# Three stacked attention layers on one core: score products of four heads together, opening work moved to GpSimd, maxima turned in half-height tiles

## The chip, the cores and the metric
The kernel runs on one core of one Trainium2 chip. The metric is the device time of one execution in microseconds (us), the median over the runs. TensorE (PE in the profile) multiplies, VectorE (DVE), ScalarE (ACT) and GpSimd (POOL) do the rest, and SyncE (SP) issues the transfers.

## The reference
One input x of 8 batches, 256 rows, 160 columns, and one context of 8 batches, 512 rows, 256 columns, pass through:

```
layer 0:  q = x Wq^T, k/v from the first 77 context rows (text) and, with other weights, from the other 435 (ip)
          20 heads of width 8, softmax over the text keys and over the ip keys apart, the two results added
          x = (text + ip) Wo^T + bo + x
layer 1:  n = layernorm(x) ; x = x + self_attention(n)         20 heads of width 64, 256 keys
          n = layernorm(x) ; x = x + cross_attention(n, ctx)   20 heads of width 64, 512 keys
          n = layernorm(x) ; x = x + (a * gelu(gate)) W2 + b2  with h = n W1 + b1 = (a, gate)
```

All in fp32. Products that need it are made of high and low parts (x = hi + lo, each rounded for one pass of TensorE).

## The kernel before, in words
The program is written engine by engine, without a scheduler: each engine walks its own list, and semaphores tie them. Four stages follow one another: layer 0 (`narrow_attention_layer`, tag l0, names `l_`), self attention (`self_attention_layer`, a1), cross attention (a2), feed forward (ff). The profile writes `a_` for a1 and for a2.

**Layer 0** takes 40 steps t: 8 batches b of 5 groups u, a group being four heads. A step has four parts s = 0 to 3. The pipeline is three deep: in step t the scores of group t are made (`score`, L1511), the exponentials of group t-2 are prepared from turned scores (`turned_scores`, L1526, then `exp` on ScalarE, L1705), and group t-3 is multiplied with the values (`weighted_sums`, L1593). A head's keys and queries lie in 32 partitions, so one score product is 32 rows by 128 queries by 512 keys. Part s makes one query tile (s // 2) of one pair of heads (s % 2): two products side by side into the two banks of `pscores[s % 2]`. VectorE reduces them to maxima (`maximum`, L1820, two reductions a part: text keys and ip keys), after which those banks are free: `score(g, s)` waits for `max_done` of the part two before it. After the four parts the maxima are turned by TensorE (`turn_max`, L1605, in part 2 of the next step) and placed into the queries by VectorE (`place_max`, L1827), between its maxima of parts 2 and 3. `PLAN` and `FIRST_PLAN` say in which parts the projections of the next batch are made (`project`, parts 1 and 3; names q, ip, text, rest, v0 to v3), and where the output of a finished batch is made ("out", part 1 of u = 2). `finish` spreads the reciprocals of a batch's sums in three pieces s0, s1, s2 (L1611), multiplied by VectorE (L1840); `invert` (L1834) makes the reciprocals, in part 3 of u = 3. Two batches ahead GpSimd splits the inputs (`split_inputs`, L1925 to L1928) and rounds the stacked keys and queries of the group three steps ahead (`round_stack`, L1951 and L1952); VectorE subtracts one small piece of it, 32 rows by 256 (`low_rest`, L1772, in part 1 of u = 4).

**Before the first step** all eight projections of batch 0 are made, in a bank each (`FIRST`).

**The opening of a1** runs in the last ten steps of layer 0 (OPEN = step 30): its weights are split into high parts (ScalarE, L595), low parts (GpSimd, L773) and the low rows of the rest (VectorE, L679), and the first layernorm is made (statistics and bias on VectorE, scaled by ScalarE). All three weights are loaded from step 24.

**Self attention** takes 40 steps d as well. In each, TensorE makes queries and keys (L514), scores (L472), turned scores (L492 to L498), weighted sums (L541, L546), turns the maxima (`turn_max`, L563: two transposes of 128 by 128 into one bank) and makes the values (L523). ScalarE copies the turned maxima into `neg_t` (`place_max`).

The tiles' places in memory are a table of addresses (`AT`).

## Time and profile before

| | us |
|---|---|
| median of 3 runs | 1612.28 |
| the three runs | 1616.55, 1592.74, 1612.28 |
| the profiled execution | 1618.48 |
| its span in the trace | 1616.7 |
| TensorE busy in it | 1544.4 (96%) |
| VectorE busy | 1106.0 (68%) |
| ScalarE busy | 776.6 (48%) |
| GpSimd busy | 419.1 (26%) |
| mean granted clock of TensorE | 0.959 |

Layer 0 fills the span from the start to about 385 us, self attention to about 800 us, cross attention to about 1530 us, feed forward the rest. Busy TensorE means that one of its instructions was open, not that the array worked at its peak. The granted clock is a share of 2.4 GHz; a stretch stands at 1.0 or at 0.5 (1.2 GHz), and a window over both shows a mean.

### The profile page before, as it was taken

What the parts mean: (1) busy time and instruction counts of PE and PEld (TensorE: products, weight loads), DVE (VectorE), ACT (ScalarE), POOL (GpSimd) and SP (SyncE); (2) the same over time, 40 slices, a digit from 0 to 9 for tenths busy, and PEclk for the clock granted to TensorE, in tenths of its full rate; (3) what the DMA queues carried; (4) which work ended last, traced back from release to release, by engine and by line L of the source; (5) the groups of instructions that cost most, each with busy time, mean ns of one, the idle gap of its engine ahead of it and who ended that gap; (6) DMA issues with size and microseconds to landing.
All of it is one profiled execution on the core that took longest, in us unless ns stands there. A gap on an engine that the chain in (4) does not pass through costs nothing.

```text
span 1616.7 us, 40554 instructions
## 1 busy us (share of the span) xinstructions
PE 1544.4 (96%) x17808; PEld 1206.9 (75%) x17808; DVE 1106.0 (68%) x1531; ACT 776.6 (48%) x1062; POOL 419.1 (26%) x375
## 2 busy tenths in 40 slices
PE   7999999998999999999999999999999999999988
PEld 5666656654788888788777877878887887877788
DVE  6777777655677777667567667676667667676666
ACT  4665656555445544556335444444444444443433
POOL 3333323320123222334312212221122222121300
PEclk7999989658999999999999999999999999999999
DMA  5322241100000020000201010101000020000000
GB/s 154 90 58 57 58 153 41 41 3 2 22 2 2 2 92 2 6 2 2 53 22 28 2 28 2 28 2 28 2 1 28 2 70 2 2 2 1 2 13 20
DMA packets 27211, 45.50 MB, mean 28 GB/s; under 512 B 7393, under 2 KB 15521, under 8 KB 26657
## 3 DMA queue, kind: packets, MB, share of 16 engines
q1 hardware_dynamic: 27040, 42.96, 9.1%
q8 instruction: 139, 2.28, 0.6%
q14 instruction: 32, 0.25, 0.1%
HBM read 29.51 MB, written 1.31 MB: 19 GB/s over the span
## 4 chain that ended last, share of the span: by engine, by line
PE 73%; DVE 9%; issue 6%; ACT 5%; POOL 3%; SPq 2%; DMA 1%; POOLq 0%; ACTq 0%; DVEq 0%
PE a_pj L994 7%; PE a_pj L982 6%; PE l_px L1593 5%; PE a_pj L514 4%; PE a_pv L1016 4%; PE a_px L1016 4%; PE l_pscore L1511 3%; PE a_px L555 3%; PE a_pv L541 3%; PE a_px L1031 2%; PE a_pscore L926 2%; PE a_pj L523 2%; PE l_pst L1526 2%; PE a_pst L947 2%; PE a_px L541 2%
## 5 line engine op out<-in xcount | busy, mean ns | idle before, releaser
L1251 POOL TENSOR_TENSOR a_key_sum<-a_probs 128x512 f32<-128x512 f32 x120 | 160.0, 1338 | 469.9 <-ACT a_probs L1084 469.9
L1163 DVE TENSOR_REDUCE a_negmax<-a_pscore 128x2 f32<-128x1024 f32 x160 | 195.7, 1223 | 105.6 <-PE a_pscore L926 105.4
L1084 ACT ACTIVATE a_probs<-a_pst 128x1024 f32<-128x1024 f32 x160 | 164.0, 1025 | 168.3 <-PE a_pst L953 167.7
L1820 DVE TENSOR_REDUCE l_negmax<-l_pscore 128x2 f32<-128x154 f32 x320 | 204.0, 685 | 57.9 <-PE l_pscore L1511 57.0
L1705 ACT ACTIVATE l_probs<-l_pst 128x1024 f32<-128x1024 f32 x160 | 163.9, 1024 | 112.1 <-PE l_pst L1526 111.6
L767 POOL TENSOR_TENSOR a_key_sum<-a_probs 128x1024 f32<-128x1024 f32 x40 | 96.0, 2401 | 243.3 <-ACT a_probs L601 243.3
L686 DVE TENSOR_REDUCE a_negmax<-a_pscore 128x4 f32<-128x1024 f32 x80 | 97.7, 1221 | 50.8 <-PE a_pscore L472 50.8
L994 PE MATMUL a_pj<-a_wv_hi,a_ct 128*128 128x256 f32 x640 | 111.1, 285 | 0.8
L1593 PE MATMUL l_px<-l_probs,l_v 128*32 128x256 f32 x1280 | 101.0, 440 | 4.9 <-DVE l_ot L1840 4.8
L1188 DVE RECIPROCAL a_recip<-a_pv 128x256 f32<-128x256 f32 x40 | 70.2, 1756 | 45.4 <-PE a_pv L1022 45.4
L601 ACT ACTIVATE a_probs<-a_pst 128x1024 f32<-128x1024 f32 x80 | 81.9, 1023 | 39.8 <-PE a_pst L498 37.7
L698 DVE RECIPROCAL a_recip<-a_pv 128x256 f32<-128x256 f32 x40 | 70.3, 1757 | 43.2 <-PE a_pv L546 43.0
L947 PE MATMUL a_pst<-a_qh,a_kh 64*128 64x256 f32 x640 | 95.4, 293 | 2.4 <-ACT a_probs L1084 1.6
L1511 PE MATMUL l_pscore<-l_k,l_q 32*128 32x512 f32 x320 | 88.1, 558 | 6.7 <-DVE l_negmax L1820 6.7
L982 PE MATMUL a_pj<-a_ct,a_wk_hi 64*128 64x512 f32 x640 | 92.6, 407 | 1.7 <-DVE a_ql L1151 1.1
L951 PE MATMUL a_pst<-a_ql,a_kh 64*128 64x256 f32 x640 | 91.3, 280 | 0.0
L953 PE MATMUL a_pst<-a_neg_t,a_sel 64*128 64x256 f32 x640 | 91.2, 279 | 0.0
L949 PE MATMUL a_pst<-a_qh,a_kl 64*128 64x256 f32 x640 | 91.1, 279 | 0.0
L994 PEld LDWEIGHTS a_pj<-a_wv_hi,a_ct 128*128 128x128 f32 x640 | 89.1, 189 | 2.3 <-DVE a_kl L1151 2.3
L1073 ACT ACTIVATE a_neg_t<-a_pscore 128x256 fp32r<-128x256 f32 x40 | 15.3, 383 | 148.4 <-PE a_pscore L1039 148.4
L1073 ACT ACTIVATE a_v<-a_pj 128x1024 f32<-128x1024 f32 x40 | 41.0, 1026 | 92.2 <-PE a_pj L994 92.2
L1016 PE MATMUL a_pv<-a_probs,a_v 128*32 128x256 f32 x1280 | 84.7, 382 | 0.0
(236 smaller groups left out, 3664.9 us busy)
## 6 DMA issues: line engine op xcount, KB each, us to landing
l_ct<-in_ctx_t SPq DMA_DIRECT2D x8, 512.0 KB, 3.8
l_k_stack<-l_k_hi SPq DMA_DIRECT2D x64, 64.0 KB, 2.1
a_ct<-in_ctx_t SPq DMA_DIRECT2D x8, 512.0 KB, 5.0
a_ct<-in_ctx_t SPq DMA_DIRECT2D x16, 256.0 KB, 5.6
l_q_stack<-l_q_hi SPq DMA_DIRECT2D x80, 32.0 KB, 1.9
...
```

What stands on the lines that cost most here:

```text
L686: nc.vector.tensor_reduce(to, pscore[:].rearrange("p h (q k) -> p h q k", q=QT), AX.X, ALU.max, negate=True).then_inc(max_done, 1)
L947: mm(pst[:, h, to], kh[OWN[h], kb, i, kt], qh[OWN[h], qb, i, :], start=True, stop=False)
L982: last = mm(pj[:, t, :], wk[hw][OWN[t], s, u * P:(u + 1) * P], cts[b % 2][OWN[t], hc, s, :], start=k == 0, stop=k == len(C_ROWS) - 1)
L994: last = mm(pj[:, kt // 2, (kt % 2) * STEP_COLS:(kt % 2 + 1) * STEP_COLS], cts[b % 2][:, hc, 2 * s, kt * P:(kt + 1) * P], wv[hw][:, s, u * ...
L1016: mm((pv, px)[x][t * 32:(t + 1) * 32, 0:SQ], v[:, e % 2, kt, t * D1 + x * 32:t * D1 + (x + 1) * 32], probs[:, t, kt, :], start=kt == 0, st ...
L1084: nc.scalar.activation(probs[:, 2 * i:2 * i + 2, 2 * n:2 * n + 2, :], pst[:].rearrange("p h (k q) -> p h k q", k=2), ACT.Exp, scale=SCALE) ...
L1163: nc.vector.tensor_reduce(to, pscore[:], AX.X, ALU.max, negate=True).then_inc(max_done, 1)
L1251: nc.gpsimd.tensor_tensor(key_sums[n][:, two], probs[:, two, 2 * n, :], probs[:, two, 2 * n + 1, :], ALU.add).then_inc(half_summed, 1)
L1511: last = mm(pscores[s % 2][:, h, :], q4[rows, u, qt * P:(qt + 1) * P], k4[rows, u, :], start=True, stop=True)
L1593: last = mm(px[j * ROWS:(j + 1) * ROWS, 0:SQ], vs[m % 2][:, kt, GROUP * u + j, :], probs[g % 2][:, j, kt, :], start=kt == 0, stop=kt == KT ...
L1705: nc.scalar.activation(probs[g % 2][:, 2 * pair:2 * pair + 2, 2 * n:2 * n + 2, :], pst[:].rearrange("p h (k q) -> p h k q", k=2), ACT.Exp, ...
L1820: last = nc.vector.tensor_reduce(to[:, :, k], pscores[s % 2][:, :, keys], AX.X, ALU.max, negate=True)
```

## The change
It has four parts. They share one new table of addresses.

1. **Scores of four heads together.** In steps 3 to 34 of layer 0, `score(t, s)` and `score(t, s + 1)` are issued in direct sequence in parts 0 and 2, and not in parts 1 and 3: the four products of one query tile, one for each head of the group, into all four score banks. Their waits stay as they are: the second pair waits for the maxima of the part before.
2. **The start of layer 0.** The values v1, v2, v3 of batch 0 are made in step 0 instead of before it, and those of batch 1 with its other projections in steps 0 to 2 (`EARLY`; before: steps 0, 2, 3 and 4), the values of batch 1 in the bank `px`. The spreading s0 goes into the bank `pj` in place of `px`. The small subtraction of `low_rest` goes from VectorE to GpSimd (`split_rest`, behind `split_inputs`).
3. **The end of layer 0.** The opening of a1 starts at step 24 in place of 30. High parts of wq and wk, the low rows of all three weights, the first bias and the low part of the first normed input go to GpSimd; the high parts of wv stay on ScalarE, in six copies of 640 columns in place of three of 1280; wv is loaded seven steps later than wq and wk.
4. **Turned maxima of a1.** Four transposes of 64 partitions by 128 into two banks, two for each query tile, in place of two of 128 by 128.

The core of the diff:

```diff
@@ PairedNorm: two new helpers
+    def pool_bias(self, pool, m):
+        pool.wait_ge(self.xhat_ready, m + 1)
+        pool.wait_ge(self.small_in, 32)
+        self.nc.gpsimd.tensor_tensor(self.xs[:, m], self.xs[:, m], self.rows[:], ALU.add).then_inc(self.biased, 1)
+
+    def pool_lo(self, pool, m, nt):
+        pool.wait_ge(self.n_hi, m + 1)
+        self.nc.gpsimd.tensor_tensor(nt[:, 1], self.n32[:], nt[:, 0].bitcast(FP32),
+                                     ALU.subtract).then_inc(self.n_ready, 1)
...
@@ self_attention_layer: which weights are made when
+    WV_HI = [(11, 0), (11, 2), (12, 0), (12, 1), (13, 0), (13, 1)]
+    WV_HALF = dram["wv"].shape[2] // 2
...
@@ self_attention_layer, tensor: turn_max
-                last = nc.tensor.transpose(pscore[:, 0, qt * P:(qt + 1) * P], negmax[:, e % 2, qt, :], ident)
+                for h in range(2):
+                    last = nc.tensor.transpose(pscore[:, h, qt * D1:(qt + 1) * D1], negmax[OWN[h], e % 2, qt, :],
+                                               ident[OWN[h], OWN[h]])
@@ self_attention_layer, scalar: place_max
-            copy(neg_t[:, e % 2, :], pscore[:, 0, 0:SQ]).then_inc(max_placed, 1)
+            copy(neg_t[:, e % 2, :].rearrange("p (t h q) -> p h t q", t=QT, h=2),
+                 pscore[:, :, 0:P].rearrange("p h (t q) -> p h t q", t=QT)).then_inc(max_placed, 1)
@@ self_attention_layer, scalar: opening(k, s)
-            if (k, s) == (0, 0):
-                act.wait_ge(loaded[0], 32)
-                copy(wq.hi[:], wq.raw[:]).then_inc(w_hi, 1)
-            if (k, s) == (0, 2):
-                copy(wq.rest[:], wq.raw_rest[:]).then_inc(w_hi, 1)
-            if (k, s) == (2, 0):
-                act.wait_ge(wq_done, 4)
-                act.wait_ge(loaded[1], 32)
-                copy(wk.hi[:], wk.raw[:]).then_inc(w_hi, 1)
-            if (k, s) == (2, 2):
-                copy(wk.rest[:], wk.raw_rest[:]).then_inc(w_hi, 1)
-            if (k, s) == (4, 0):
-                ln.act_xhat(act, 0, (0,))
-            if (k, s) == (4, 2):
-                ln.act_xhat(act, 0, (1,))
-            if (k, s) == (6, 0):
+            if (k, s) == (8, 1):
+                ln.act_xhat(act, 0)
+            if (k, s) in WV_HI:
+                i = WV_HI.index((k, s))
+                if i == 0:
+                    for moved in ahead["moved"]:
+                        act.wait_ge(*moved)
+                    act.wait_ge(loaded[2], 32)
+                of, raw = (wv.hi[:, i // 2], wv.raw[:, i // 2]) if i < 4 else (wv.rest, wv.raw_rest)
+                half = slice(i % 2 * WV_HALF, (i % 2 + 1) * WV_HALF)
+                copy(of[:, half], raw[:, half]).then_inc(wv_hi, 1)
+            if (k, s) == (13, 2):
                 act.wait_ge(*ahead["normed"])
                 ln.act_hi(act, 0, nts[0])
-            if (k, s) == (6, 1):
-                act.wait_ge(wk_done, 4)
-                for moved in ahead["moved"]:
-                    act.wait_ge(*moved)
-                act.wait_ge(loaded[2], 32)
-                copy(wv.hi[:, 0], wv.raw[:, 0]).then_inc(w_hi, 1)
...
@@ self_attention_layer, vector: opening(k, s)
-            if k == 1 and s in (0, 2):
-                dve.wait_ge(w_hi, 2)
-                low_rows(wq, s // 2).then_inc(wq_done, 1)
...
-            if (k, s) == (3, 3):
+            if (k, s) == (3, 0):
                 ln.dve_stats(dve, 0)
-            if (k, s) == (5, 0):
-                ln.dve_bias(dve, 0)
-            if (k, s) == (7, 0):
-                dve.wait_ge(w_hi, 7)
-                low_rows(wv, 0).then_inc(wv_done, 1)
-            if (k, s) == (7, 2):
-                ln.dve_lo(dve, 0, nts[0])
...
@@ self_attention_layer, gpsimd: opening(k)
+            def high(w, at):
+                pool.wait_ge(loaded[at], 32)
+                nc.gpsimd.tensor_copy(w.hi[:], w.raw[:])
+                nc.gpsimd.tensor_copy(w.rest[:], w.raw_rest[:]).then_inc(w_hi, 1)
+                pool.wait_ge(w_hi, at + 1)
...
+            def low_rows(w, done):
+                for h in range(2):
+                    rows = slice(h * D1 + REST, (h + 1) * D1)
+                    pool.wait_ge(done, 2 + h)
+                    nc.gpsimd.tensor_tensor(w.rest[rows], w.raw_rest[rows], w.rest[rows].bitcast(FP32),
+                                            ALU.subtract).then_inc(done, 1)
+                pool.wait_ge(done, 4)
+
+            for at, (w, done, first) in enumerate(((wq, wq_done, 1), (wk, wk_done, 6))):
+                if k == first:
+                    high(w, at)
+                if k == first + 2:
+                    for s in range(2):
+                        low(w, s).then_inc(done, 1)
+                    low_rows(w, done)
+            if k == 4:
                 ln.pool_setup(pool)
                 ln.pool_rstd(pool, 0)
-            if k == 6:
+            if k == 9:
+                ln.pool_bias(pool, 0)
+            if k == 11:
                 nc.gpsimd.memset(negmax[:], 0.0).then_inc(negmax_zeroed, 1)
+                nc.gpsimd.memset(ones[:], 1.0).then_inc(ones_set, 1)
+            if k in (12, 13):
+                pool.wait_ge(wv_hi, 2 * (k - 12) + 2)
+                low(wv, k - 12).then_inc(wv_done, 1)
+            if k == 14:
+                pool.wait_ge(wv_hi, 6)
+                low_rows(wv, wv_done)
+                ln.pool_lo(pool, 0, nts[0])
...
@@ narrow_attention_layer: the table of projections
-    FIRST_PLAN = {0: ("ip", "text"), 1: (None, None), 2: ("q", "rest"), 3: ("v0", "v1"), 4: ("v2", "v3")}
-    PLAN = {0: ("ip", "text"), 1: ("q", "rest"), 2: (None, "v0"), 3: ("v1", "v2"), 4: ("v3", None)}
...
+    EARLY = {(0, 0): ("v1", 0), (0, 1): ("v2", 0), (0, 2): ("ip", 1), (0, 3): ("v3", 0),
+             (1, 0): ("text", 1), (1, 1): ("v0", 1), (1, 2): ("v1", 1), (1, 3): ("v2", 1),
+             (2, 0): ("v3", 1), (2, 1): ("q", 1), (2, 3): ("rest", 1)}
+    PLAN = {(0, 1): "ip", (0, 3): "text", (1, 1): "q", (1, 3): "rest", (2, 3): "v0", (3, 1): "v1", (3, 3): "v2",
+            (4, 1): "v3"}
...
+        if (u, s) == (4, 3) and 0 <= b - 1 < B - 1:
+            return ("s0", b - 1)
...
@@ narrow_attention_layer, tensor: project and part
+            if what == "s0":
+                pe.wait_ge(recip_done, m + 1)
...
+                spread_recip(0, pj).then_inc(pj_ready, 1)
+                return
...
         def part(t, s):
-            if here(t):
+            if here(t) and not V_LAG <= t < ALL - GROUPS:
                 score(t, s)
+            elif here(t) and s % 2 == 0:
+                score(t, s)
+                score(t, s + 1)
             if here(t - T_LAG):
                 turned_scores(t - T_LAG, s)
...
@@ narrow_attention_layer: the rest's low rows go from vector to gpsimd
-        def low_rest(m):
-
-            dve.wait_ge(in_hi, 2 * m)
-            lo = nts[m % 2][2 * REST:EXT, 2]
-            subtract(lo, x32[2 * REST:EXT, 1], lo.bitcast(FP32)).then_inc(rest_ready, 1)
...
-            if s == 1 and t % GROUPS == GROUPS - 1 and t // GROUPS + 2 < B:
-                low_rest(t // GROUPS + 2)
...
+        def split_rest(m):
+            pool.wait_ge(in_ready, m)
+            lo = nts[m % 2][2 * REST:EXT, 2]
+            subtract(lo, x32[2 * REST:EXT, 1], lo.bitcast(FP32)).then_inc(rest_ready, 1)
+            pool.wait_ge(rest_ready, m)
...
             if u == 3 and b + 2 < B:
                 split_inputs(b + 2)
+                split_rest(b + 2)
@@ build
-        OPEN, LOAD, FF_OPEN = S0 - 10, 24, S2 - 5
+        OPEN, FF_OPEN = S0 - 16, S2 - 5
...
-                if d == LOAD:
-                    own["load_weights"]()
-                if d == LOAD + 7:
+                if d == OPEN:
+                    own["load_weights"](range(2))
+                if d == OPEN + 7:
                     own["load_small"]()
+                    own["load_weights"]([2])
```

**TensorE in layer 0, a step with u = 1** (L1511 is now L1535, L1526 L1550, L1593 L1638, L1536 L1560, L1605 L1650). `l_pscore<-l_k,l_q` are score products, `l_pst` turned scores, `l_px<-l_probs,l_v` weighted sums, `l_pj<-identity,l_negmax` the turned maxima. Before:

```order
L1511 MATMUL l_pscore<-l_k,l_q 128x512 x2
L1526 MATMUL l_pst<-l_q,l_k 128x256 x4
L1593 MATMUL l_px<-l_probs,l_v 32x256 x8
L1511 MATMUL l_pscore<-l_k,l_q 128x512 x2
L1526 MATMUL l_pst<-l_q,l_k 128x256 x4
L1536 MATMUL l_pj<-l_nt,l_wq 128x256 x8
L1511 MATMUL l_pscore<-l_k,l_q 128x512 x2
L1526 MATMUL l_pst<-l_q,l_k 128x256 x4
L1593 MATMUL l_px<-l_probs,l_v 32x256 x8
L1605 MATMUL l_pj<-identity,l_negmax 128x128 x2
L1511 MATMUL l_pscore<-l_k,l_q 128x512 x2
L1526 MATMUL l_pst<-l_q,l_k 128x256 x4
```

and now:

```order
L1535 MATMUL l_pscore<-l_k,l_q 128x512 x4
L1550 MATMUL l_pst<-l_q,l_k 128x256 x4
L1638 MATMUL l_px<-l_probs,l_v 32x256 x8
L1550 MATMUL l_pst<-l_q,l_k 128x256 x4
L1560 MATMUL l_pj<-l_nt,l_wq 128x256 x8
L1535 MATMUL l_pscore<-l_k,l_q 128x512 x4
L1550 MATMUL l_pst<-l_q,l_k 128x256 x4
L1638 MATMUL l_px<-l_probs,l_v 32x256 x8
L1650 MATMUL l_pj<-identity,l_negmax 128x128 x2
L1550 MATMUL l_pst<-l_q,l_k 128x256 x4
```

Two of the four score groups of a step have moved up to the other two.

**VectorE in layer 0, from u = 3 to u = 4 of a batch**, before (L1834 the reciprocal, L1772 the small subtraction, L1820 the maxima, two reductions a part):

```order
L1820 TENSOR_REDUCE l_negmax<-l_pscore 128x2 x2
L1834 RECIPROCAL l_recip<-l_den 40x256
L1820 TENSOR_REDUCE l_negmax<-l_pscore 128x2 x4
L1772 TENSOR_TENSOR l_nt<-l_x,l_nt 32x256
L1820 TENSOR_REDUCE l_negmax<-l_pscore 128x2 x2
L1827 TENSOR_TENSOR l_q<-l_q,l_pj 128x256
```

The subtraction is now on **GpSimd**, behind the other splits of the same input (L1965 was L1919):

```order
L1971 CAST l_ct<-l_ct 128x1024
L1973 CAST l_nt<-l_x 128x256
L1974 CAST l_nt<-l_x 128x256
L1965 TENSOR_TENSOR l_ct<-l_ct 128x1024
L1965 TENSOR_TENSOR l_nt<-l_x,l_nt 128x256
L1965 TENSOR_TENSOR l_nt<-l_x,l_nt 32x256
L2005 CAST l_k<-l_k_stack 128x512
```

On GpSimd it stands ahead of the rounding of a later group's keys.

**ScalarE in step 32 of layer 0**, before: the copy `a_wk_hi` stands between exponentials and waits for GpSimd's low parts of wq (`a1_wq_done`).

```order
L1667 ACTIVATE l_rest_lo<-l_pj 128x512
L1705 ACTIVATE l_probs<-l_pst 128x2x512 [waits l0_st_ready,l0_px_ready]
L595 ACTIVATE a_wk_hi<-a_raw_wk 128x1280 [waits a1_loaded1,a1_wq_done]
L1705 ACTIVATE l_probs<-l_pst 128x2x512 [waits l0_st_ready] x2
L1667 ACTIVATE l_sums<-l_px 128x256 [waits l0_px_ready]
L595 ACTIVATE a_wk_rest<-a_raw_wk_rest 128x640
```

and now the same place has the four copies of the first layernorm:

```order
L1750 ACTIVATE l_probs<-l_pst 128x2x512 [waits l0_st_ready,l0_px_ready]
L1750 ACTIVATE l_probs<-l_pst 128x2x512 [waits l0_st_ready]
L276 ACTIVATE a_ln_xhat<-xs,a_ln_shift,a_ln_rstd 128x256 [waits a1_ln_shift_ready]
L280 ACTIVATE a_ln_xhat<-xs,a_ln_shift,a_ln_rstd 128x128
L276 ACTIVATE a_ln_xhat<-xs,a_ln_shift,a_ln_rstd 128x256
L280 ACTIVATE a_ln_xhat<-xs,a_ln_shift,a_ln_rstd 128x128
L1750 ACTIVATE l_probs<-l_pst 128x2x512 [waits l0_st_ready]
```

No copy of ScalarE waits for wq any more; the wait for `a1_ln_shift_ready` is for work that GpSimd has in its list four steps earlier.

## Rows read from the trace of the kernel before

**Rows 1.** The page's parts 1 and 2: busy engines, granted clock in 40 slices.
```profile
PE 1544.4 (96%) x17808; PEld 1206.9 (75%) x17808; DVE 1106.0 (68%) x1531; ACT 776.6 (48%) x1062; POOL 419.1 (26%) x375
...
PEclk7999989658999999999999999999999999999999
```

**Rows 2.** Windows of the trace; their order: length, busy PE, PEld, DVE, ACT, POOL, clock, DMA.
```profile
core 0: us, PE busy (x) PEld busy (x) DVE busy (x) ACT busy (x) POOL busy (x), PEclk, DMA share, GB/s
...
147.83:188.46 40.63, 39.97 (x371) 26.48 (x370) 31.60 (x52) 26.71 (x38) 14.24 (x19) 1.00 0.15 38
...
165.32:179.43 14.11, 14.11 (x139) 8.91 (x138) 12.24 (x21) 10.30 (x16) 6.20 (x9) 1.00 0.29 73
...
127.21:147.83 20.62, 18.25 (x144) 11.25 (x144) 16.39 (x23) 10.43 (x15) 7.59 (x10) 0.83 0.30 87
...
172.15:188.46 16.31, 15.65 (x143) 9.97 (x142) 14.22 (x23) 10.45 (x15) 7.64 (x10) 1.00 0.25 62
...
212.77:234.81 22.04, 19.82 (x144) 11.79 (x144) 16.37 (x23) 10.65 (x15) 7.60 (x10) 0.77 0.38 119
...
259.15:280.22 21.07, 18.82 (x144) 11.58 (x143) 16.28 (x23) 12.44 (x17) 7.59 (x10) 0.84 0.19 48
...
288.45:361.68 73.23, 69.40 (x425) 42.57 (x425) 41.72 (x69) 37.49 (x49) 22.95 (x25) 0.58 0.09 24
...
18.95:57.27 38.32, 35.54 (x211) 22.12 (x210) 27.64 (x46) 17.89 (x27) 15.38 (x23) 0.69 0.47 136
```

**Rows 3.** Timeline of TensorE in step 11: start, length, engine, line, operation.
```profile
102.89 0.50 PE L1511 MATMUL l_pscore<-l_k,l_q 32*128 32x512 f32 x2
...
104.56 0.50 PE L1511 MATMUL l_pscore<-l_k,l_q 32*128 32x512 f32 x2
...
104.89 0.41 PE L1526 MATMUL l_pst<-l_q,l_k 32*128 32x256 f32 x4
...
106.37 0.50 PE L1511 MATMUL l_pscore<-l_k,l_q 32*128 32x512 f32 x2
...
108.40 0.50 PE L1511 MATMUL l_pscore<-l_k,l_q 32*128 32x512 f32 x2
...
111.08 0.50 PE L1511 MATMUL l_pscore<-l_k,l_q 32*128 32x512 f32 x2
```

**Rows 4.** Timeline of VectorE in the same step.
```profile
106.91 1.29 DVE L1820 TENSOR_REDUCE l_negmax<-l_pscore 128x2 f32<-128x154 f32 x2 [0.53 <-PE l_pscore L1511]
...
108.51 0.42 DVE L1827 TENSOR_TENSOR l_q<-l_q,l_pj 128x256 fp32r<-128x256 f32 x1 [0.30 <-PE l_pj L1605]
...
108.94 1.29 DVE L1820 TENSOR_REDUCE l_negmax<-l_pscore 128x2 f32<-128x154 f32 x2
```

**Rows 5.** Timeline where four score multiplies stand together.
```profile
361.66 0.52 PE L1511 MATMUL l_pscore<-l_k,l_q 32*128 32x512 f32 x4
...
361.99 0.40 PE L1526 MATMUL l_pst<-l_q,l_k 32*128 32x256 f32 x4
```

**Rows 6.** Timeline, steps 13 to 15: VectorE, then TensorE.
```profile
127.45 1.73 DVE L1834 RECIPROCAL l_recip<-l_den 40x256 f32<-40x256 f32 x1
...
131.55 2.59 DVE L1772 TENSOR_TENSOR l_nt<-l_x,l_nt 32x256 fp32r<-32x256 f32 x1
...
135.62 0.49 PE L1511 MATMUL l_pscore<-l_k,l_q 32*128 32x512 f32 x2 [1.07 <-DVE l_negmax L1820]
```

**Rows 7.** Timeline around the long slow stretch: POOL, ScalarE, TensorE.
```profile
291.84 3.04 POOL L773 TENSOR_TENSOR a_wq_lo<-a_raw_wq,a_wq_hi 128x640 fp32r<-128x640 f32 x2
...
294.92 1.27 ACT L595 ACTIVATE a_wk_hi<-a_raw_wk 128x1280 fp32r<-128x1280 f32 x1 [4.36 <-POOL a_wq_lo L773]
...
297.15 0.79 PE L1526 MATMUL l_pst<-l_q,l_k 32*128 32x256 f32 x4 [2.70 <-ACT l_probs L1705]
```

**Rows 8.** Timeline of TensorE around turned maxima of the second layer.
```profile
503.41 0.44 PE L563 MATMUL a_pscore<-identity,a_negmax 128*128 128x128 f32 x2
...
503.78 0.50 PE L523 MATMUL a_pj<-a_wv_hi,a_nt 64*128 64x256 f32 x4
```

181 lines of the change are left out of this document (95 added, 86 removed), and 49 rows, old and new, of the table AT.

## The prediction

> **What bounds the kernel now.** The page first: TensorE has an instruction open for 96% of the span, VectorE for 68%, and the granted clock is full in most slices but not in those of the first 400 us, layer 0 [rows 1]. So the question for layer 0 is what holds TensorE back there, and for self attention only how much work TensorE is given. The windows answer the first. Each runs from the first score product of a step to that of a later one [rows 2]. Five consecutive steps, 16 to 20, with every kind of work in them, take 40.63 us at full clock with TensorE open for 39.97 of it: this is the undisturbed pace, 8.13 us a step. Against it stand two kinds of disturbed stretch. Steps 14 and 15, 24 and 25, 29 and 30 take 20.62, 22.04 and 21.07 us, where the same two places of a batch (steps 19 and 20) take 16.31. And steps 32 to 37 take 73.23 us, six steps at 12.2, with a mean clock of 0.58: some 61 of the 73 us at 1.2 GHz.
>
> The timeline names the causes. In steps 13 to 15 VectorE spends 1.73 us on the reciprocal and then 2.59 us on a subtraction of 32 rows by 256 [rows 6]; the maxima behind it come late, TensorE stands for 1.07 us, and the clock falls in that window (0.83). What the subtraction should cost is bounded by the 0.42 us of a VectorE operation of 128 by 256 in the undisturbed step [rows 4]. Before the long stretch ScalarE waits 4.36 us, with exponentials queued behind the wait, for low parts that GpSimd makes late, then copies for 1.27 us, and TensorE stands for 2.70 us [rows 7]. This stall is what precedes the fall of the clock.
>
> **The sum, part by part,** against the profiled execution of 1618.5 us.
>
> *Small subtraction off VectorE.* The three disturbed pairs return to 16.31: 20.62 + 22.04 + 21.07 - 3 x 16.31 = **-14.8 us**. On GpSimd it lies beside everything; GpSimd is busy 14.24 of 40.63 us of a batch, and the rounding behind it is for a group three steps ahead. By the Trainium skill (SBUF — State Buffer, Who interferes with whom) a VectorE instruction with two inputs in SBUF contends with a GpSimd instruction that reads it; the 2.59 us are what that would look like, and on GpSimd's own queue the piece can't meet it.
>
> *The opening of a1.* ScalarE no longer waits for wq. At the undisturbed pace steps 32 to 37 take 6 x 8.13 = 48.8, so -24.4 us. That is pessimistic by a little, since steps 35 and 36 have no projection, and optimistic by the six half copies of wv, each half of 1.27 us, of which ScalarE can't hide all. I take **-24 us**. GpSimd gets the copies and low parts. At 1.52 us for 128 by 640 (half of 3.04, [rows 7]) that is, with two low parts, two pieces of low rows of the same width and 1920 columns of copies at no more than that price, 4 x 1.52 + 3 x 1.52 = 10.6 us each for wq and wk. They are spread over three steps of some 24 us each, in which GpSimd was busy a third of the time, so they fit. wv's eight pieces of 640 columns (12.2 us) must be done before step 40; they can start at step 36, 4 x 8.13 = 32 us earlier.
>
> *Scores of four heads together.* The trace has the case once: four products start together and take 0.52 us, two take 0.50, and the next instruction starts 0.33 us after them in either case [rows 3, 5]. So a second pair is free, and TensorE gives up 0.33 us in parts 1 and 3, 0.66 a step. Part 1 can't use its share fully, since its turned scores then wait for the exponential of part 0; I give it 0.1. So TensorE alone would gain 0.4 us a step, 32 x 0.4 = 13 us, and 32 x 0.66 = 21 at the very most. But the four banks now come free together. In the second half of a step VectorE starts 0.54 us after the products (106.37 to 106.91), makes a maximum, waits for the turned maxima, places them, and ends the last maximum at 108.94 + 1.29 = 110.23 [rows 3, 4]. With 0.2 us for the semaphore the next step's four products can start 4.05 us after those of part 2. The first half of a step is bounded the same way, 0.54 + 2 x 1.29 + 0.1 = 3.2 us. The undisturbed steps 18 and 19 take 14.11 us together [rows 2]. By the new chain step 18 takes 3.2 + 4.05 = 7.25; the reciprocal of 1.73 us, until now swallowed by a queue of two parts, delays the next maxima by 1.0 us beyond their 0.54, so step 19 takes 4.2 + 4.05 = 8.25; together 15.5, 1.4 more than now. The other three steps of a batch are long enough to gain: 3 x 0.4, and some 0.4 for s0 no longer standing in the bank of the sums. A batch is -1.6 + 1.4: **0 us**, between -13 and +1.4 x 6.4 = +9.
> The Trainium skill (TensorEngine Tiling (Array Packing), PSUM Bottleneck) says that tiling speeds up TensorE but not the emptying of PSUM, which may then bound. By its general claim of a gain the term would be -13, by this warning 0; the rows above carry the warning.
>
> *The start.* Steps 0 to 4 take 38.32 us at a clock of 0.69 [rows 2]. The work is the same, moved to where VectorE's maxima leave TensorE idle, and VectorE loses a small piece. If the clock stays as it is I see **-2 us**; 5 x 8.13 = 40.7 would be no gain at all, full clock throughout might give -8.
>
> *The end of layer 0.* VectorE loses the low rows of wv and the first low part, 2 to 4 us of its work where it was behind: **-3 us**, between 0 and -6.
>
> *Turned maxima of a1.* Now 0.37 us lie between the first transpose (128 rows) and the values (64 rows) that follow it [rows 8]. Half-height tiles run in pairs, each streams 64 columns, and the change of tile height before the values goes. Four 64-row products of 256 columns, two pairs, are open for 0.50 us in the same rows; two pairs of 64 columns take no less than a quarter of that, 0.12, and at worst the 0.37 of now. I take 0.19, nearer to the small end since the column count is what shrinks: a gain of 0.18 us. It counts in 32 of 40 steps; in the other eight the layernorm's full transposes follow and the change of height merely moves. TensorE is dense there: **-5.5 us**, between 0 and -8. ScalarE's copy out of two banks instead of one is as long, beside TensorE.
>
> Sum: -14.8 - 24 + 0 - 2 - 3 - 5.5 = -49.3, so 1569 for the profiled execution. The median of the runs shown is 6 us below it, and the fastest 26 below. That one probably had no long slow stretch, so I don't subtract the whole 6 from a version that should have none either. **Forecast 1567 us.**
>
> **Rivals.**
> *A. TensorE's own saving comes through in full,* because the chain of maxima is shorter than I add it up: -13 in place of 0, 1554 us. For it: VectorE is busy for 31.60 us of a batch's 40.63 [rows 2], so its work alone would fit into the shorter time. Against it: the latencies between the engines, which make the 4.05 us. Chance 0.12.
> *B. The clock still falls for short times.* Step 19's pattern leaves TensorE idle for about 1 us, as long as the 1.07 us at which it fell [rows 6]. The fast stretch of steps 16 to 20 had no such gap. Six falls at some 2.5 us: 1582 us. Chance 0.13.
> *C. The long slow stretch stays,* since the last batch is thin on TensorE and something else starts it (the ScalarE copies of wv, say): +24, 1591 us. Chance 0.12.
> *D. Slower than before.* The clock falls at the new gap behind a reciprocal and, as in steps 32 to 37, does not come back. At 12.2 instead of 8.1 us a step, 12 such steps eat the whole gain of 49 us; over all 32 steps it would be +131, so 1567 + 131 = 1698 us. For it: nothing but a dense block ended that stretch. Against it: in every batch a dense "out" or projection comes within three steps, and three short falls did end there. The Trainium skill (TensorE: Matmul & The Clock Gate, Why this matters for your kernels) warns of gaps between bursts of products; the rows agree, the clock being 0.77 to 0.84 in the windows with a gap. Chance 0.05.
> *E. The four products don't run together,* the second pair waiting for its maximum each time, and TensorE pays 0.33 us more at the places where it bounds: 16 x 0.33, 1572 us. Chance 0.03; it changes little.
>
> **How the numbers follow.** Forecast 0.55. Its own range is the bounds of its terms taken together loosely, 1555 to 1582. The range of eight in ten takes in A, B and most of C: 1550 to 1597. Two per cent, about what a measurement can tell from no change, is 32 us: below 1580 lie the forecast but for its upper edge, A, E and half of B, 0.72; between 1580 and 1644 the rest of B and C, 0.23; above only D, 0.05.
>
> **What would show each step right or wrong.** Step times in the timeline: the pairs of steps 14/15, 24/25 and 29/30 within 1 us of 16.3 and no VectorE operation of 2.5 us between maxima; steps 32 to 37 near 49 us at a clock of 1.0, with ScalarE never waiting for GpSimd. Four score products in one row of about 0.52 us, followed by turned scores. TensorE waiting for `l_negmax` in front of the score products of parts 0, most in u = 4: if those waits are small, A holds. In the half behind part 2 about 4.05 us between products. In self attention the distance of turned maxima shorter by 0.2 us than before and L563's successors starting within 0.2 us. The forecast is wrong if the clock row shows fives outside the first slice or two, or if VectorE's two-input work turns up elsewhere beside GpSimd's longer queue.

## The result, and the profile after

Over 20 runs each the changed kernel took 1596.56 us (1578.20 to 1611.51), the kernel before 1610.91 (1592.74 to 1628.07). The ratio is 0.9912, 95% interval [0.9884, 0.9941]: faster by 0.9%, less than the 2% that the chances spoke of. Ratios and intervals, here and in the experiments, leave out executions more than 1.5% over the fastest of the same kernel (on two of the chips 12 of 25 and 12 of 23 of the kernel before), so a ratio need not be that of the medians of all runs beside it. The forecast was 1567. The profiled execution took 1598.35 us, 20.1 less than that of before. The page's busy engines and granted clock, to be read beside [rows 1]:

```profile
PE 1512.6 (95%) x17888; PEld 1190.1 (75%) x17888; DVE 1082.2 (68%) x1515; ACT 773.1 (48%) x1061; POOL 439.1 (28%) x395
...
PEclk7799999977999999999999999999999999999999
```

The long slow stretch is shorter (`77` where `658` stood), and the one at the start is longer (`77` in place of `79`). The windows of the changed kernel, from the first score product of a step to that of a later one: steps 16 to 20; 14 and 15; 29 and 30; 32 to 37; 0 to 4; 5 to 9; and step 38 up to the first turned maxima of self attention.

```profile
core 0: us, PE busy (x) PEld busy (x) DVE busy (x) ACT busy (x) POOL busy (x), PEclk, DMA share, GB/s
153.40:193.35 39.95, 38.08 (x371) 24.73 (x370) 30.34 (x51) 26.72 (x38) 14.79 (x20) 1.00 0.21 58
137.53:153.40 15.87, 15.00 (x144) 9.32 (x144) 13.47 (x22) 10.31 (x15) 8.19 (x11) 1.00 0.25 63
...
257.36:276.24 18.88, 16.52 (x144) 10.12 (x143) 13.46 (x22) 10.51 (x15) 14.72 (x18) 0.91 0.22 57
284.35:343.86 59.51, 50.67 (x427) 31.03 (x426) 35.06 (x57) 35.00 (x49) 23.48 (x24) 0.80 0.20 62
18.86:63.92 45.06, 42.56 (x227) 27.89 (x228) 25.33 (x44) 18.17 (x29) 14.92 (x21) 0.59 0.42 121
63.92:105.41 41.49, 38.22 (x349) 22.94 (x349) 29.73 (x49) 27.66 (x39) 15.75 (x23) 0.91 0.19 53
343.86:386.57 42.71, 34.55 (x319) 21.14 (x318) 20.80 (x37) 22.48 (x28) 6.79 (x6) 0.80 0.01 2
```

Against [rows 2]: the disturbed pairs have become 15.9 us at full clock, but for steps 29 and 30 (18.9). Steps 32 to 37 went from 73.2 to 59.5, not to 49. Steps 0 to 4 went from 38.3 up to 45.1 at a clock of 0.59, and steps 5 to 9 from 36.9 to 41.5.

**The stall that is left in step 35.** The timeline of SyncE, then ScalarE, then TensorE:

```profile
314.01 0.59 SPq L1460 DMA_DIRECT2D l_q_stack<-l_q_lo  x1
...
316.07 0.74 ACT L611 ACTIVATE a_wv_hi<-a_raw_wv 128x640 fp32r<-128x640 f32 x1 [6.11 <-DMA l_q_stack<-l_q_lo]
...
317.77 0.79 PE L1550 MATMUL l_pst<-l_q,l_k 32*128 32x256 f32 x4 [6.24 <-ACT l_probs L1750]
```

The first copy of wv waits until the stacks' last transfers have landed (`moved`), since its tile lies over theirs. SyncE issues the last one at 314.0. ScalarE stands for 6.1 us with the exponentials behind it, TensorE for 6.2, and the clock is at half from 314 to 338 us. In the kernel before the same wait stood in step 36 and cost nothing.

**The start.** TensorE of the changed kernel:

```profile
18.86 0.50 PE L1535 MATMUL l_pscore<-l_k,l_q 32*128 32x512 f32 x2 [1.56 <-DVE l_q L1942]
19.29 0.90 PE L1573 MATMUL l_pst<-l_wc,l_ct 128*128 128x160 f32 x6
...
20.54 1.57 PE L1573 MATMUL l_pst<-l_wc,l_ct 128*128 128x160 f32 x6
...
26.34 1.57 PE L1573 MATMUL l_px<-l_wc,l_ct 128*128 128x160 f32 x6
```

Step 0 begins when VectorE has rounded the first queries, at 18.9 us in both kernels. The three values of batch 0, 4.0 us, now lie behind that moment, two of them at half clock.

**Four score products together**, second half of step 18, TensorE and VectorE:

```profile
173.91 0.51 PE L1535 MATMUL l_pscore<-l_k,l_q 32*128 32x512 f32 x4
...
174.46 1.29 DVE L1867 TENSOR_REDUCE l_negmax<-l_pscore 128x2 f32<-128x154 f32 x2 [0.63 <-PE l_pscore L1535]
...
176.18 0.42 DVE L1874 TENSOR_TENSOR l_q<-l_q,l_pj 128x256 fp32r<-128x256 f32 x1 [0.43 <-PE l_pj L1650]
...
176.52 1.28 DVE L1867 TENSOR_REDUCE l_negmax<-l_pscore 128x2 f32<-128x154 f32 x2
...
177.48 0.87 PE L1535 MATMUL l_pscore<-l_k,l_q 32*128 32x512 f32 x4
```

The products run together (0.51 us). The next ones start 3.57 us later and before the second maximum has ended (177.80): only the second pair of products waits for it.

**Turned maxima of self attention**, against [rows 8]:

```profile
487.69 0.34 PE L578 MATMUL a_pscore<-identity,a_negmax 64*128 64x64 f32 x4
487.83 0.48 PE L537 MATMUL a_pj<-a_wv_hi,a_nt 64*128 64x256 f32 x4
```

0.14 us lie between the two starts, 0.37 before. A step takes 7.82 in place of 8.06 us.

### The profile page after: what moved, and what is told of

Read it like the earlier page. It is cut to its first block, busy times and chain, and to the rows that moved or that the text cites. A ratio compares the mean times of both kernels' runs of the same rounds, so it can differ in the third digit from the quotient of the medians.

```text
span 1596.6 us, 40717 instructions
## 1 busy us (share of the span) xinstructions
PE 1512.6 (95%) x17888; PEld 1190.1 (75%) x17888; DVE 1082.2 (68%) x1515; ACT 773.1 (48%) x1061; POOL 439.1 (28%) x395
## 4 chain that ended last, share of the span: by engine, by line
PE 71%; ACT 8%; DVE 8%; issue 6%; POOL 3%; SPq 2%; DMA 1%; ACTq 0%; POOLq 0%; DVEq 0%
PE a_pj L999 7%; PE a_pj L987 6%; PE a_pj L528 4%; PE a_pv L1021 4%; PE a_px L1021 4%; PE a_px L569 3%; PE l_px L1638 3%; PE a_pv L555 2%; PE a_px L1036 2%; PE l_pst L1550 2%; ACT l_probs L1750 2%; PE a_pscore L931 2%; PE a_pst L952 2%; PE a_px L555 2%; PE a_pj L537 2%
## 5 line engine op out<-in xcount | busy, mean ns | idle before, releaser
L1550 PE MATMUL l_pst<-l_q,l_k 32*128 32x256 f32 x640 | 80.2, 330 | 19.7 <-ACT l_probs L1750 19.2
L701 DVE RECIPROCAL a_recip<-a_pv 128x256 f32<-128x256 f32 x40 | 70.3, 1757 | 41.4 <-PE a_pv L560 40.9
L1550 PEld LDWEIGHTS l_pst<-l_q,l_k 32*128 32x128 f32 x640 | 57.2, 202 | 51.4 <-ACT l_probs L1750 43.6
L1638 PE MATMUL l_px<-l_probs,l_v 128*32 128x256 f32 x1280 | 95.2, 419 | 0.0
L1078 ACT ACTIVATE a_neg_t<-a_pscore 128x256 fp32r<-128x256 f32 x40 | 15.4, 384 | 148.5 <-PE a_pscore L1044 148.5
```

Of the source, the lines that this page charges most:

```text
L1550: last = mm(pst[:, h, i * SQ:(i + 1) * SQ], k4[rows, u, kt * P:(kt + 1) * P], q4[rows, u, :], start=True, stop=True)
L1638: last = mm(px[j * ROWS:(j + 1) * ROWS, 0:SQ], vs[m % 2][:, kt, GROUP * u + j, :], probs[g % 2][:, j, kt, :], start=kt == 0, stop=kt == KT ...
```

## The experiments

Each experiment is the changed kernel or the kernel before with the edit shown, as its expectation says. The table gives microseconds by stretch of one profiled execution of each kernel: steps of layer 0, from step 38 to the first turned maxima of self attention (end), from there to the last (a1). The last two columns are the median of all runs, and the ratio to the kernel before, run on the same chip, with its 95% interval.

| kernel | 0-4 | 5-9 | 10-31 | 32-37 | end | a1 | median | ratio |
|---|---|---|---|---|---|---|---|---|
| before | 38.3 | 36.9 | 194.3 | 73.2 | 39.3 | 397.6 | 1610.9 | 1 |
| the change | 45.1 | 41.5 | 178.9 | 59.5 | 42.7 | 390.7 | 1596.6 | 0.9912 [0.9884, 0.9941] |
| start_back | 36.7 | 37.4 | 176.7 | 59.6 | 42.7 | 390.3 | 1585.4 | 0.9874 [0.9838, 0.9909] |
| wv_later | 46.3 | 40.4 | 177.3 | 45.4 | 41.2 | 391.4 | 1579.7 | 0.9841 [0.9755, 0.9926] |
| rest_alone | 36.5 | 37.1 | 176.9 | 67.8 | 49.1 | 396.4 | 1602.9 | 0.9993 [0.9954, 1.0032] |
| quads_alone | 37.4 | 43.5 | 180.3 | 58.3 | 49.1 | 396.5 | 1603.5 | 1.0038 [0.9992, 1.0083] |
| both | 36.0 | 37.4 | 177.6 | 45.4 | 41.2 | 391.6 | 1570.6 | 0.9775 [0.9740, 0.9809] |
| both_by_part | 35.1 | 37.2 | 177.6 | 45.0 | 41.2 | 391.6 | 1570.5 | 0.9777 [0.9736, 0.9818] |
| batch0_ahead | 32.2 | 44.7 | 178.6 | 59.4 | 44.3 | 392.3 | 1590.6 | 0.9882 [0.9837, 0.9926] |
| both_pool | 34.6 | 37.4 | 175.8 | 45.4 | 39.1 | 391.7 | 1577.4 | 0.9801 [0.9759, 0.9843] |
| maxima_alone | 36.1 | 49.6 | 190.8 | 63.2 | 49.1 | 392.3 | 1604.3 | 1.0017 [0.9971, 1.0063] |
| rest_wk_later | 36.4 | 37.1 | 176.9 | 60.7 | 49.1 | 396.5 | 1595.6 | 0.9935 [0.9893, 0.9978] |
| both_spread | 33.5 | 40.9 | 177.4 | 45.4 | 40.0 | 391.1 | 1571.9 | 0.9809 [0.9768, 0.9849] |
| rest_open_order | 35.1 | 37.1 | 177.0 | 50.3 | 49.1 | 396.2 | 1583.1 | 0.9829 [0.9770, 0.9888] |

### start_back

```diff
-    EARLY = {(0, 0): ("v1", 0), (0, 1): ("v2", 0), (0, 2): ("ip", 1), (0, 3): ("v3", 0),
-             (1, 0): ("text", 1), (1, 1): ("v0", 1), (1, 2): ("v1", 1), (1, 3): ("v2", 1),
-             (2, 0): ("v3", 1), (2, 1): ("q", 1), (2, 3): ("rest", 1)}
+    EARLY = {(0, 1): ("ip", 1), (0, 3): ("text", 1), (2, 1): ("q", 1), (2, 3): ("rest", 1),
+             (3, 1): ("v0", 1), (3, 3): ("v1", 1), (4, 1): ("v2", 1), (4, 3): ("v3", 1)}
```

The bank of the values of batch 1, one wait of TensorE and VectorE's marks go back with the table.

> The changed kernel, with only the start of layer 0 as before: all eight projections of batch 0 made before step 0, those of batch 1 in steps 0, 2, 3 and 4, the ones of VectorE set before step 0. Theory 1 (the moved projections cost): in the changed kernel steps 0 to 4 take 45.1 us against 38.3 before, because the values v1, v2, v3 of batch 0 were made in a time in which TensorE waited anyway (step 0 starts at 18.9 us in both kernels), and now lie in steps that run at half clock. Then steps 0 to 4 return to 38 to 39 us and the whole loses 6 to 7 us: 0.996 of the changed kernel, 0.987 of the kernel before. Theory 2 (the four score products together, already used in steps 3 and 4, cost it): steps 0 to 4 stay above 43 us. Steps 5 to 9 (41.5 us, before 36.9) should stay as they are under both.

Theory 1 held for steps 0 to 4 (36.7 us), and more came: steps 5 to 9 returned as well (37.4), against what both theories expected. TensorE at the beginning:

```profile
16.45 0.84 PE L1572 MATMUL l_px<-l_wc,l_ct 128*128 128x160 f32 x6
18.95 0.51 PE L1534 MATMUL l_pscore<-l_k,l_q 32*128 32x512 f32 x4 [1.67 <-DVE l_q L1941]
```

All values of batch 0 are done at 17.3, and TensorE still waits 1.67 us for the rounding: they were free there.

### batch0_ahead

```diff
-    EARLY = {(0, 0): ("v1", 0), (0, 1): ("v2", 0), (0, 2): ("ip", 1), (0, 3): ("v3", 0),
+    EARLY = {(0, 2): ("ip", 1),
```

> The changed kernel with only the values v1, v2, v3 of batch 0 made before step 0 again; batch 1's projections stay in steps 0 to 2. It splits the 12.5 us that steps 0 to 9 lost. Theory 1a (work taken out of free time): the three projections were open for 4.0 us in step 0, at half clock for two of them; that much comes back in steps 0 to 4 (45.1 to 41), and steps 5 to 9 keep their 41.5 us. Theory 1b (steps 3 and 4 are left thin by batch 1's projections moving to steps 0 to 2, and the clock falls at 58 us and again at 85 us): the rest, steps 3 to 9, stays slow here, with a half-clock stretch near 55 to 62 us. If instead steps 5 to 9 return to 37.4, the loss there came from batch 0's values alone.

```profile
19.82:51.98 32.16, 26.39 (x210) 16.13 (x210) 24.92 (x44) 17.07 (x27) 9.82 (x16) 0.95 0.51 150
51.98:96.66 44.68, 40.56 (x350) 23.93 (x350) 29.74 (x49) 28.01 (x40) 20.23 (x27) 0.85 0.22 60
```

Theory 1b held: steps 5 to 9 stay slow, with a fall of the clock at 56 us. Theory 1a had the place but a third of the size: without the three values steps 0 to 4 run at a clock of 0.95 and give back 12.9 us, not 4. Steps 5 to 9 take 3.2 us more than in the changed kernel, which places batch 1's projections in the same steps; so what these 3.2 us come from is not shown. Of the 12.5 us that separate the change from start_back, 9.7 come back here in all.

### both_spread

`both` (below) with another table for batch 1:

```diff
+    EARLY = {(0, 2): ("ip", 1), (1, 0): ("text", 1), (1, 2): ("v0", 1),
+             (2, 1): ("q", 1), (2, 3): ("rest", 1), (3, 1): ("v1", 1), (3, 3): ("v2", 1), (4, 1): ("v3", 1)}
```

> The mended kernel with another table for batch 1's projections: ip, text and v0 in steps 0 and 1, q and rest in step 2, v1, v2, v3 in steps 3 and 4. The kernel with only batch 0's values ahead took 32.2 us for steps 0 to 4, but 44.7 for steps 5 to 9, because nothing was left for steps 3 and 4 and the clock fell at 56 us. Theory 1: with work left in both places steps 0 to 9 take 70 to 72 us, in place of 73.4 in the mended kernel: 1568 us, 0.998 of it. Rival (where the clock falls in the first 60 us is not set by this): 73 to 77 us, no gain.

The rival held: steps 0 to 9 take 74.4 us, both 73.4. What steps 0 to 4 gained went at a fall of the clock at 88 us, although steps 3 and 4 now had projections in them.

### wv_later

```diff
-    WV_HI = [(11, 0), (11, 2), (12, 0), (12, 1), (13, 0), (13, 1)]
+    WV_HI = [(12, 0), (12, 1), (12, 2), (12, 3), (13, 0), (13, 1)]
```

> The changed kernel, with the six copies of wv's high parts starting one step later (step 36, the first four in one step). Theory 1: in step 35 ScalarE stands for 6.1 us because its first copy waits for the last transfers of the key and query stacks, which SyncE issues only in that step; the exponentials are queued behind it, and the stall also starts the half clock of 314 to 338 us. Then step 35 falls from 16.5 to about 8 us, steps 32 to 37 from 59.5 to about 49 us, and the whole gains 10 us: 0.985 of the kernel before. Theory 2 (the last batch is thin for TensorE and the clock falls there anyway): step 35 falls to about 10 us but steps 36 and 37 stay at 10.9 and 8.4, a gain of 6 us. Theory 3 (another wait takes its place, the weights' transfer itself or GpSimd behind a later copy): less than 3 us.

```profile
283.64:329.03 45.39, 42.59 (x425) 27.16 (x424) 34.91 (x57) 34.72 (x49) 22.27 (x24) 1.00 0.27 82
```

Theory 1, and a little more: 14.1 us off steps 32 to 37, which now run at full clock throughout. The one line moves the profiled execution by 15.6 us.

### rest_alone

```diff
-            if s == 1 and t % GROUPS == GROUPS - 1 and t // GROUPS + 2 < B:
-                low_rest(t // GROUPS + 2)
...
+                split_rest(b + 2)
```

> The kernel before, with only the small subtraction of 32 rows by 256 moved from VectorE to GpSimd. Theory 1 (the prediction's step): the three disturbed pairs of steps (14/15, 24/25, 29/30: 20.6, 22.0, 21.1 us) return to 16.3, the clock stays full in them, 14.8 us gained, 0.991 of the kernel before, and everything after step 32 stays. Rival: the pairs are disturbed by something else, such as the reciprocal of 1.73 us, which stays; then they stay above 19 us and the time is that of before.

Windows of steps 14 and 15, 32 to 37, and the end:

```profile
126.14:141.90 15.76, 15.64 (x144) 9.96 (x144) 13.90 (x22) 10.46 (x15) 8.20 (x11) 1.00 0.25 62
...
270.25:338.00 67.75, 63.00 (x426) 38.61 (x426) 41.86 (x70) 37.18 (x49) 22.95 (x25) 0.67 0.10 26
338.00:387.12 49.12, 40.32 (x320) 24.42 (x319) 23.22 (x40) 21.87 (x27) 0.97 (x3) 0.65 0.01 2
```

The cause is shown: all three pairs take 15.8 us, steps 10 to 31 lose 17.4, and the eleven kernels here with the piece on GpSimd take 175.8 to 178.9 us in these steps, the three with it on VectorE 180.3 to 194.3. But the end takes 49.1 us at a clock of 0.65, in place of 39.3 at 0.91, and no gain shows in the runs (medians 1602.9 against 1608.4 on that chip; the interval of the ratio takes in 1). The five kernels here with the end of before all take 49.1 us there, and only the profiled execution of before itself does not. Whether that was chance, or came from the long slow stretch that ended 3 us ahead of step 38 in it (the clock was full again at 358 us), is not shown.

The traces show more of the cause than the prediction had. The subtraction stands in each of the steps 9, 14, 19, 24 and 29 of the kernel before, and took 0.42, 2.59, 0.42, 2.56 and 2.47 us. GpSimd and VectorE in step 14 [rows 6], then in step 19:

```profile
131.50 2.37 POOL L1919 TENSOR_TENSOR l_ct<-l_ct 128x1024 fp32r<-128x1024 f32 x1
...
176.78 0.42 DVE L1772 TENSOR_TENSOR l_nt<-l_x,l_nt 32x256 fp32r<-32x256 f32 x1 [0.32 <-POOL l_nt L1928]
176.83 2.60 POOL L1919 TENSOR_TENSOR l_ct<-l_ct 128x1024 fp32r<-128x1024 f32 x1
```

Where GpSimd's split started 0.05 us ahead (131.50 against 131.55), VectorE's small piece took 2.59 us and its pair of steps 20.6; where VectorE was ahead by 0.05 us, the piece took 0.42 us and the pair 16.3. maxima_alone has the same layer 0 as before and hits other steps: 2.46 and 2.63 us in steps 19 and 29 (pairs of 20.7 and 20.8 us), 0.42 in steps 14 and 24 (16.2 and 16.1). So the price is that of a collision, and how many an execution has differs: three here, two there.

### quads_alone

```diff
-            if here(t):
+            if here(t) and not V_LAG <= t < ALL - GROUPS:
                 score(t, s)
+            elif here(t) and s % 2 == 0:
+                score(t, s)
+                score(t, s + 1)
```

> The kernel before, with only the score products of four heads issued together in parts 0 and 2 of steps 3 to 34. Theory 1 (what the changed kernel shows): an undisturbed batch of five steps takes 39.9 in place of 40.6 us, but in steps 5 to 9, where a batch is short of other work and the order by parts let them run in 36.9 us, the chain of maxima behind four banks bounds and they take 40 to 41.5. Over all steps that is a gain of 4 x 0.7 less a loss of 3 to 4.6: no change, 1.000 within 0.003, if the disturbed pairs stay as they are. Rival 1: the longer steps 5 to 9 of the changed kernel come from the moved projections or tables and not from the quads; then they take 37 us here. Rival 2: with the subtraction still on VectorE the chain is longer, more of the clock falls: slower by 10 us or more.

Steps 5 to 9 take 43.5 us, but not by the chain of maxima, as I had it: the window shows a clock of 0.81, and with the subtraction gone (start_back, both) the same steps take 37.4 with the products together and 37.2 by parts. Nor does the table tie that clock to the products: maxima_alone, which makes them by parts, takes 49.6 us in these steps. Alone the products together show no gain (1.0038, interval with 1 in it). That steps 10 to 31 take 180.3 us and not 194.3 is not theirs either: in this execution the subtraction, still on VectorE, took 0.42 us in steps 14, 19, 24 and 29 alike, without one collision.

### both and both_by_part

both is the changed kernel with the edits of start_back and wv_later; both_by_part takes besides

```diff
-            if here(t) and not V_LAG <= t < ALL - GROUPS:
-                score(t, s)
-            elif here(t) and s % 2 == 0:
-                score(t, s)
-                score(t, s + 1)
+            if here(t):
+                score(t, s)
```

> The changed kernel with both mends: the start as in the kernel before, and wv's copies one step later. The two cures lie 200 us apart and share no resource. Theory 1 (independent): steps 0 to 9 take 74 us (86.6 in the changed kernel), steps 32 to 37 take 45.4 (59.5), so 26.6 us less than the changed kernel, some 1570 us, 0.975 of the kernel before. Theory 2 (the clock hands the time on: a half-clock stretch that is removed at one place comes at another, as the kernel before with only the small subtraction moved showed, whose end of layer 0 became 9.8 us longer): 10 us of it come back behind step 38, 1580 us.

> The same mended kernel, but with the score products issued part by part as in the kernel before. Theory 1 (the prediction's term of 0 for the four together): an undisturbed batch takes 40.05 us by parts (the kernel before with the subtraction moved) against 39.92, so layer 0 becomes 0.5 to 1 us longer, nothing measurable: 1.000 within 0.002 of the mended kernel. Rival (the four products together are what fills TensorE and holds the clock up in thin steps): steps 5 to 9 or 35 to 39 fall to half clock at more places, 5 to 10 us slower. Second rival (they cost: a chain of maxima behind four banks): 3 us faster.

The two mends add up (1570.6 us, 26 under the change by the medians, 22 by the ratios), with nothing handed back at the end. The products together are worth nothing that shows: 1570.5 without them. An undisturbed batch, steps 15 to 19, of both, then of both_by_part:

```profile
132.17:172.10 39.93, 38.04 (x373) 24.74 (x372) 30.35 (x51) 26.73 (x38) 14.64 (x21) 1.00 0.21 58
```

```profile
131.52:171.42 39.90, 39.90 (x371) 26.55 (x370) 31.20 (x51) 26.70 (x39) 15.01 (x21) 1.00 0.21 59
```

TensorE is open for 1.9 us less, and the batch is as long. The time saved turns into waits, most of them for ScalarE's exponentials and only one for the maxima. TensorE's waits in the window of both (us in total, times, longest):

```profile
PE l_pst L1549 <- ACT l_probs L1749: 1.1, 5, 0.4
PE l_pscore L1534 <- DVE l_negmax L1866: 0.4, 1, 0.4
```

The same view of both_by_part names no wait.

### both_pool

```diff
-                if k == first + 2:
+                if k == first + (3 if at == 0 else 2):
...
+                if i == 2:
+                    sp.wait_ge(wq_done, 4)
```

> The mended kernel, and GpSimd's low parts and low rows of wq (6.3 us) one step later, behind the split of the last batch's inputs and not ahead of it. In the changed kernel step 30 took 11.1 us, in the one with the old start 9.0, against 8.06 in other batches, with the projection of the keys waiting 1.5 us for GpSimd's split. Theory 1: step 30 returns to 8.1 us; a gain of 1 to 3 us against the mended kernel. Rival: GpSimd is then late with the rounding for step 32, which takes 9.2 us now and becomes longer by as much.

Step 30 of both, then of both_pool:

```profile
251.94:261.72 9.78, 7.94 (x77) 5.21 (x76) 6.45 (x12) 5.22 (x7) 7.31 (x12) 1.00 0.20 51
```

```profile
251.34:259.39 8.05, 7.88 (x75) 5.21 (x74) 6.45 (x12) 5.23 (x7) 7.60 (x9) 1.00 0.19 49
```

The cause of step 30 is shown (9.8 to 8.1 us, step 32 stays at 9.2). The gain is not: two of its six runs took 1564 us, four 1576 to 1580, at clocks of 0.987 and 0.974 to 0.977. That stays inconclusive.

### maxima_alone

The edit is the `turn_max` and `place_max` of the change, put into the kernel before.

> The kernel before, with only the turned maxima of self attention in four transposes of 64 partitions. Theory 1 (the prediction's term, corrected by the trace of the changed kernel, where 0.14 us lie between the first transpose and the values in place of 0.37): a step of self attention takes 7.82 in place of 8.06 us, the stretch from the first to the last turned maxima 390.5 to 391.5 us in place of 397.6, and the whole gains 6 to 7 us, 0.996 of the kernel before. Rival (the shorter self attention of the changed kernel came from its clock or its tables): the stretch stays at 397 us.

The stretch of self attention went from 397.6 to 392.3 us: 5.3 us, near the forecast's 5.5 and under the 6 to 7 expected here. Its profiled execution lost more than that elsewhere (steps 7 to 9 at half clock), and ten runs can't show 5 us: 1.0017 with a half-width of 0.0046, which is 7 us.

### rest_wk_later and rest_open_order

rest_alone, with ScalarE's copies of wk a step later, and VectorE's low rows too; then with the statistics and GpSimd's shift of the layernorm earlier as well.

```diff
-            if (k, s) == (2, 0):
+            if (k, s) == (3, 0):
                 act.wait_ge(wq_done, 4)
...
-            if (k, s) == (2, 2):
+            if (k, s) == (3, 2):
```

```diff
-            if (k, s) == (3, 3):
+            if (k, s) == (2, 3):
                 ln.dve_stats(dve, 0)
...
             if k == 3:
+                ln.pool_setup(pool)
+                ln.pool_rstd(pool, 0)
                 pool.wait_ge(w_hi, 3)
```

> The kernel before, with the small subtraction on GpSimd and with ScalarE's copies of wk (and VectorE's low rows of them) one step later, nothing else. Theory 1 (one wait at the head of ScalarE's queue starts the long slow stretch; the work of the opening, where it lies, is nearly free): ScalarE no longer stands 4.4 us in step 32, steps 32 to 37 take 45 to 49 us in place of 67.8 (with the subtraction moved) and 73.2 (before), and the kernel is as fast as the mended changed kernel but for the turned maxima and the start: 1580 to 1585 us, 0.985. Theory 2 (the stretch comes from the opening's work on ScalarE and VectorE, which the changed kernel gave to GpSimd): the steps stay above 60 us, 0.998.

> The kernel before with the small subtraction on GpSimd and the copies of wk a step later, and now the statistics of the first layernorm at the end of step 32 in place of 33 and GpSimd's square root and shift ahead of wk's low parts, not behind them. In the kernel without this, the stall of step 32 was gone but ScalarE stood for 4.97 us in step 34, waiting for the shift, with the exponentials behind it; steps 32 to 37 took 60.7 us. Theory 1 (only the waits at the head of ScalarE's queue hold the steps back, and each one that goes shows the next): with the shift early, steps 33 and 34 take 7.3 us each, and steps 32 to 37 take 45 to 50 us, as in the mended changed kernel (45.4) although ScalarE and VectorE still do all the work of the opening; 1575 to 1585 us. Theory 2 (the moved work itself matters): still above 55 us with a half-clock stretch, 1590 us or more.

In the first, steps 32 and 33 take 9.3 and 7.3 us, about as undisturbed ones, but steps 32 to 37 take 60.7 and not 45 to 49: the next wait in ScalarE's queue takes over.

```profile
293.39 0.60 ACT L277 ACTIVATE a_ln_xhat<-xs,a_ln_shift,a_ln_rstd 128x256 f32<-128x256 f32 x1 [4.97 <-POOL a_ln_shift L269]
...
295.33 0.79 PE L1526 MATMUL l_pst<-l_q,l_k 32*128 32x256 f32 x4 [3.15 <-ACT l_probs L1705]
```

In the second that wait is 1.26 us, and the window of steps 32 to 37 is:

```profile
268.56:318.86 50.30, 45.84 (x426) 28.82 (x425) 41.46 (x70) 36.31 (x49) 23.49 (x25) 0.97 0.13 34
```

50.3 us against rest_alone's 67.8, by order alone, with all the opening's work still on ScalarE and VectorE; both reaches 45.4. Between the two lie what is left of ScalarE's wait (1.26 us) and a fall of the clock of 3.4 us; what each costs is not shown. The whole, at 0.9829, is at least as fast as the change at 0.9912, and has nothing of the change but the moved subtraction.

## Why the prediction was wrong, point by point

Three of the six terms came out near their size (the subtraction, the four products, the turned maxima). The start went the other way, the opening gave little more than half, and the end can't be told from one execution. In all 49 us were forecast and 20 came in the profiled pair; in the medians 45 were forecast and 14 came. By stretch, against the profiled execution of before:

| step of the sum | forecast | the change | both |
|---|---|---|---|
| start, steps 0 to 4; steps 5 to 9 | -2; 0 | +6.7; +4.6 | -2.3; +0.5 |
| small subtraction and scores together, steps 10 to 31 | -14.8 | -15.4 | -16.7 |
| opening of a1, steps 32 to 37 | -24 | -13.7 | -27.9 |
| end of layer 0 | -3 | +3.4 | +1.9 |
| turned maxima of a1 | -5.5 | -6.9 | -5.9 |
| everything else | 0 | +1.0 | +0.7 |
| sum | -49.3 | -20.1 | -49.7 |

The mended kernel comes to the forecast's sum against that execution, in part by luck: the opening and the subtraction gave 6 us more than forecast, the end took 5 more. In the medians it is 38 us under before, since before's profiled execution is 10 us over the median of its runs on that chip, and that of both 2 under its own. The prediction read its terms from this one execution, with its three collisions, and took all but 4 us of them over to the median.

*The start failed.* The prediction said that "the work is the same, moved to where VectorE's maxima leave TensorE idle". It did not ask what the place cost that the work came from. That place was free (a wait of 1.67 us for VectorE is left behind it), and the new one is bound by TensorE at half clock. start_back shows the whole of it, 12.5 us; batch0_ahead shows that batch 0's values are most of it, 9.7. Where the other 2.8 come from stays open: steps 3 and 4 left thin were my reading, but both_spread puts work there and gains nothing.

*The opening half failed.* The term took away one wait of ScalarE and priced the copies that stay, not their own wait. For the copy of wv the prediction named only its duration; what it waits for is a transfer that SyncE issues in the same step, and the change moved the copy a step ahead of it. wv_later gives 14.1 us back, more than the 10.3 that were missing. Rival C was near (a stretch started by ScalarE's copies of wv), with the stall as its cause, not the copies' length; but the stretch kept 10 us and not 24, so that 1591 lies near the measured 1597 is luck. That GpSimd's longer queue would fit was wrong at one place, step 30, by 1.7 to 3 us.

*The subtraction was right* as a cause, and in this pair in size (-15.4 us). What the prediction missed is that the 2.59 us are a matter of who starts first: the same piece took 0.42 us in step 19, inside the stretch that it called undisturbed. -14.8 is the price of three collisions in one execution, and maxima_alone had two. That may be why the gain does not show in the runs of rest_alone; one profiled execution for each kernel can't show it.

*The four products were right at 0*, though by errors that cancel. Steps 18 and 19 take 6.8 and 7.8 us, not 7.25 and 8.25: I let the next products wait for the last maximum, and only their second pair does. And against both_by_part the step behind the reciprocal (19) loses 0.5 us, while the other four gain 0.1 to 0.2 each, not 0.4. TensorE's open time fell by 1.9 us a batch, 0.37 a step, where I had 0.66 given up; that part 1 would wait for ScalarE was right (1.1 us in five steps against my 0.23 a step). Of the 0.7 us that a batch is shorter than in [rows 2], 0.6 belong to the subtraction (rest_alone, 40.1).

*The end*: -3 can't be held against one number. Five kernels with before's end show 49.1 us, the eight with the changed end 39.1 to 44.3, but the profiled execution of before itself 39.3. The difference goes with the clock (0.65 in rest_alone, 0.80 in the change, 0.91 in the two that take 39 us). At that same clock of 0.91 before takes 39.3 us and both_pool 39.1, so the work taken off VectorE, which the term was for, gave 0.2 us and not 3. What in the changed end holds the clock up stays open.

*The turned maxima* came out at -5.3 us alone (maxima_alone) against -5.5. The 1.6 us more in the change come in one step, which takes 9.9 us there and 11.5 in maxima_alone.

*Rivals.* A: no, TensorE's own saving became waits. B: no fall in steps 10 to 28. D: no; after each fall the clock came back. E: no, 0.51 us for four.
